# Feed-forward of a hybrid attention block: VectorE makes the inverse of the block scale from the block maximum itself

## The chip, the cores and the metric

One core of a Trainium2 chip runs the whole kernel. The metric is the device time of one execution in microseconds (us). The core has five engines that run their own instruction streams and meet at semaphores: TensorE (PE in the profile; PEld is its weight load), VectorE (DVE), ScalarE (ACT), GpSimd (POOL) and SyncE (SP), which starts the transfers.

## The reference

The input x has 2 x 2048 tokens of 128 channels. Four stages follow, each added to x behind a layer norm: an attention with landmarks, the feed-forward, a linear attention, and the same feed-forward again. The change touches the two feed-forwards alone:

```
def fp4_quant_dequant(x):                       # blocks of 16 along the last dim
    scale = jnp.max(jnp.abs(xb), axis=-1, keepdims=True) / 6.0
    scale = jnp.maximum(scale, jnp.float32(1e-12))
    xn = xb / scale
    idx = jnp.searchsorted(_MID, jnp.abs(xn))   # nearest value of a grid of 8
    q = _GRID[idx] * jnp.sign(xn) * scale

gate = fp4_linear(x, w_gate)                    # both operands quantised
y = fp4_linear(x, w_up)
h = jax.nn.silu(gate) * y                       # 352 wide
return fp4_linear(h, w_down)
```

## The kernel before

The tokens are 32 tiles of 128 tokens (a token on each partition), which stay in SBUF in X. A feed-forward, `ffn(p)` for p = 0 (the first pass) and p = 1 (the second), quantises x by quads of four tiles (8 quads, 512 columns, 32 blocks for a partition) and h by pairs of two tiles (16 pairs, 2 x 352 columns, 44 blocks). All engines walk the same loop over rounds r from -4 to 18; in round r VectorE works on pair r, POOL on the products of pair r - 1, TensorE on the down products of pair r - 2, and in an even round with q = (r + 4) / 2 below 8 the quad q is begun, in the odd round behind it moved on. So x quads are worked on up to r = 11, and in r = 12 to 15 there is h alone.

For one pair the steps are: TensorE's gate and up products (L1234, L1236), ScalarE's silu (L546), VectorE's product (`gated`, L876) into the PSUM bank of up. Then VectorE's block maximum (`absmax_h`, L880) into `hblk[:, 0]`; POOL's scale (`scales`, L254), maximum / 6 but at least 1e-12, into `hblk[:, 2]`; VectorE's reciprocal of it (`inverse`, L841) into `hblk[:, 1]`; VectorE's ratio (`ratio_h`, L886) in PSUM; ScalarE's offset |ratio| x 2^22 in bf16 (`offset_h`, L572); VectorE's clamp of the offset from below (`clamp`, L862, bf16, SBUF to SBUF) and its addition of ratio and offset (`move_h`, L895); in the next round, on POOL, the subtraction of the offset, which leaves the rounded value (`quantise_h`, L271), and the product with the scale (L274). TensorE transposes (L1247), ScalarE copies (L553), TensorE multiplies by w_down (L1255), and the residual is added: in pass 0 by POOL (L279) after a copy by ScalarE (L560), in pass 1 by VectorE straight from PSUM (L899). An x quad goes the same way: `absmax_x` (L849), L254, L841, `ratio_x` (L856), L566, L862, L869, and on POOL `quantise_x` (L261, L264).

The order of each engine is written out in its loop. VectorE in round r: gated twice, absmax_h; absmax_x (even) or clamp and move_x (odd); the residual of pair r - 2 in pass 1; inverse and ratio of h; inverse and ratio of x (even); layernorm statistics of two tiles in pass 0 (L664, L666); clamp and move_h. POOL in round r: the scale of x (even), the scale of h, quantise_h(r - 1), quantise_x (odd), then in pass 0 the residual of pair r - 3 and, in even rounds, four small layernorm steps (L326, among them a power). Semaphore counts order the engines; each step waits for what it reads and for whoever still reads what it overwrites.

Of the kernel before, what the change touches and what calls it, by code (L numbers as in the profile page):

```python
# [16 lines left out]
ALU = mybir.AluOpType  # L17
# [37 lines left out]
TIE = 1.0 - 2.0 ** -23  # L55
# [3 lines left out]
def build(nc, x_d, wqkv_d, wqkvT_d, band_d, wfc_d, bfc_d, wattn_d, battn_d, wproj_d, bproj_d,  # L59
          wg_d, wu_d, wd_d, eye_d, scaled_eye_d, tri_d, blockmask_d, headones_d, rowhead_d, valid_d, centre_d, out_d):  # L60
    with ExitStack() as ctx:
# [9 lines left out]
        s = Signals()  # L71

        def need(eng, name, value):

            if not (isinstance(value, int) and value <= 0):
                eng.wait_ge(s[name], value)
# [111 lines left out]
        def ffn_tiles(p, n):  # L188

            return p * TILES + n  # L190

        def ffn_pairs(p, n):

            return p * PN + n

        def ffn_quads(p, n):

            return p * QN + n
        def up_banks(r):

            return ps[:, 1 + 2 * (r % 2):3 + 2 * (r % 2), 0:F]
# [453 lines left out]
        def _(v):  # L655
            tt, ts, stt = nc.vector.tensor_tensor, nc.vector.tensor_scalar, nc.vector.scalar_tensor_tensor
            reduce, copy, recip = nc.vector.tensor_reduce, nc.vector.tensor_copy, nc.vector.reciprocal
# [24 lines left out]
            def by_block(t):  # L682
# [10 lines left out]
                op0=ALU.mult, op1=ALU.mult).then_inc(s["w_chain"], 1)  # L693
# [10 lines left out]
            for c in range(4):  # L704
                last = copy(out=a2[32 * c:32 * c + 32, :, :],
                            in_=ps[32 * c:32 * c + 32, c % 2, 0:U * M].rearrange("p (u m) -> p u m", m=M))
# [40 lines left out]
            with v.Fori(0, ITERS) as i:  # L747
# [9 lines left out]
                for hf in range(2):  # L757
                    v.wait_ge(s["zT_done"], 2 * i + hf + 1)
                    ts(out=zT[:, 4 * hf:4 * hf + 4, :], in0=banks(6 + hf, 1, P), scalar1=0.25, scalar2=None,
                       op0=ALU.mult).then_inc(s["zT_copied"], 1)  # L760
# [71 lines left out]
            def ffn(p):  # L832
                def pair(t):
                    return t.rearrange("p (k n) -> p k n", k=2)

                def blocks(t):
                    return t.rearrange("p k (b j) -> p k b j", j=BLK)

                def inverse(name, b, n):
                    v.wait_ge(s[name + "_scale"], n + 1)  # L840
                    recip(out=b[:, 1, :], in_=b[:, 2, :]).then_inc(s[name + "_inverse"], 1)  # L841

                def x_blocks():
                    return ps[:, X_BANK:X_BANK + 1, :]

                def absmax_x(q):
                    n = ffn_quads(p, q)
                    v.wait_ge(s["fx_norm"], n + 1)
                    reduce(out=xblk[:, 0, :].unsqueeze(1), in_=blocks(x_blocks()), axis=AX, op=ALU.max,  # L849
                           apply_absolute_value=True).then_inc(s["fx_absmax"], 1)  # L850

                def ratio_x(q):
                    n = ffn_quads(p, q)
                    inverse("fx", xblk, n)
                    v.wait_ge(s["fx_inverse"], n + 1)
                    stt(out=blocks(x_blocks()), in0=blocks(x_blocks()), scalar=TIE,  # L856
                        in1=xblk[:, 1, :].unsqueeze(1).unsqueeze(3).broadcast_to([P, 1, QD * P // BLK, BLK]), op0=ALU.mult,
                        op1=ALU.mult).then_inc(s["fx_ratio"], 1)

# [17 lines left out]

                def absmax_h(r):
                    v.wait_ge(s["f_h"], ffn_tiles(p, 2 * r + 2))
                    reduce(out=pair(hblk[r % 2][:, 0, :]), in_=blocks(up_banks(r)), axis=AX, op=ALU.max,  # L880
                           apply_absolute_value=True).then_inc(s["fh_absmax"], 1)

                def ratio_h(r):
                    n = ffn_pairs(p, r)
                    v.wait_ge(s["fh_inverse"], n + 1)
                    stt(out=blocks(up_banks(r)), in0=blocks(up_banks(r)), scalar=TIE,  # L886
                        in1=pair(hblk[r % 2][:, 1, :]).unsqueeze(3).broadcast_to([P, 2, F // BLK, BLK]), op0=ALU.mult,
                        op1=ALU.mult).then_inc(s["fh_ratio"], 1)

# [12 lines left out]
                for r in range(-FILL, PN + (4 if p == 0 else 3)):  # L902
                    q = (r + FILL) // 2
                    if 0 <= r < PN:
                        gated(2 * r)
                        gated(2 * r + 1)
                        absmax_h(r)
                    if r % 2 == 0 and q < QN:
                        absmax_x(q)
                    if r % 2 and q < QN:  # L910
                        move_x(q)
                    if p == 1 and 0 <= r - 2 < PN:
                        residual(r - 2)
                    if 0 <= r < PN:
                        inverse("fh", hblk[r % 2], ffn_pairs(p, r))
                        ratio_h(r)
                    if r % 2 == 0 and q < QN:
                        ratio_x(q)
                    if p == 0 and 0 <= r - 4 < PN:
                        v.wait_ge(s["f_x_done"], ffn_pairs(p, r - 3))  # L920
                        tile_stats(2, 2 * r - 8)
                        tile_stats(2, 2 * r - 7)
                    if 0 <= r < PN:
                        move_h(r)
# [497 lines left out]
```

## Time and profile before

| what | value |
|---|---|
| median of 3 runs | 854.62 us (854.15 to 855.4) |
| the profiled execution | 855.14 us, of which the span from the first to the last instruction is 853.3 us |
| busy over the span | PE 620.8 us (73%), PEld 445.2 (52%), DVE 543.6 (64%), ACT 296.9 (35%), POOL 317.6 (37%) |
| chain that ended last | PE 46%, DVE 30%, issue 10%, POOL 8%, ACT 5% |
| granted clock of TensorE | 0.873 of full speed |
| feed-forward of pass 0 | from about 384 to 516 us |
| feed-forward of pass 1 | from about 718 us to the end |

How to read it: one execution was recorded, and a busy engine is not yet one that bounds. The two feed-forwards are a third of the time, and which engine is late there has to be read from their own stretches. In a row of the timeline stand the start (us from the span's beginning), the duration, the engine, the source line, the operation, output <- inputs with their shapes, and in brackets how long the engine stood idle before it and for whom. A duration holds whatever an instruction stood still for once it was issued, so a longer one for the same shape tells of something outside of it.

### The profile page before, as it was taken

To read this page: it belongs to the slowest core of one execution; us is meant where nothing else is said; L and a number is where in the kernel's file an instruction comes from. 1 tells how busy PE (TensorE), PEld (TensorE's weight loads), DVE (VectorE), ACT (ScalarE), POOL (GpSimd) and SP (SyncE) were. 2 spreads that over 40 slices of the span, in tenths; PEclk is the share of its full clock that TensorE was granted. 3 is DMA by queue.
4 is the path that set the end of the run, shared out by engine and by line. 5 is a ranking of instruction groups with operands and counts; after the bars stand their busy time and mean duration, and the time that the engine had idled before them with its cause. 6 is when DMAs were issued, how large, how long until landed. Compare 5 with 4: busy or idle time off the path is not lost.

```text
span 853.3 us, 14006 instructions
## 1 busy us (share of the span) xinstructions
PE 620.8 (73%) x5231; PEld 445.2 (52%) x5231; DVE 543.6 (64%) x1078; ACT 296.9 (35%) x523; POOL 317.6 (37%) x408
## 2 busy tenths in 40 slices
PE   2467887888667477694777766698988985777675
PEld 1366784666434344692555544355655653455554
DVE  7624663333198498475889881376667765688874
ACT  2131112333243233204555542233333333545542
POOL 6540000000100000043678876345555534456654
PEclk9567999999988788797899985599999998799997
DMA  8400000000000000000000000000000000000000
GB/s 251 107 1 1 0 1 1 0 1 0 1 2 0 1 1 1 1 1 0 1 1 1 1 1 0 1 1 3 2 1 2 2 2 2 0 13 26 13 25 25
DMA packets 13675, 10.47 MB, mean 12 GB/s; under 512 B 1398, under 2 KB 12598, under 8 KB 13492
## 3 DMA queue, kind: packets, MB, share of 16 engines
q1 hardware_dynamic: 13620, 9.73, 4.1%
q8 instruction: 35, 0.57, 0.3%
q14 instruction: 20, 0.16, 0.1%
HBM read 7.63 MB, written 2.10 MB: 11 GB/s over the span
## 4 chain that ended last, share of the span: by engine, by line
PE 46%; DVE 30%; issue 10%; POOL 8%; ACT 5%; DMA 0%; ACTq 0%; DVEq 0%; POOLq 0%
PE ps L1098 6%; PE ps L1184 4%; PE ps L1318 4%; PE ps L1213 4%; PE ps L1125 3%; DVE ps L876 3%; PE ps L1337 3%; DVE r L786 2%; PE ps L1255 2%; DVE ps L886 2%; DVE hblk L880 2%; DVE hoff L862 2%; PE ps L1134 2%; DVE S L794 2%; PE ps L1142 2%
## 5 line engine op out<-in xcount | busy, mean ns | idle before, releaser
L1247 PE MATMUL ps<-eye,arena 128*128 128x128 f32 (+1 forms) x192 | 32.4, 312 | 56.4 <-POOL arena L274 56.4
L326 POOL TENSOR_TENSOR ln<-mv,lnc 128x4 f32<-128x4 f32 x64 | 13.2, 207 | 155.7 <-DVE mv L666 155.7
L345 POOL MEMSET early<- 128x2560 f32 x2 | 4.5, 2232 | 173.1 <-PE ps L1169 162.0
L1184 PE MATMUL ps<-G,xw 128*126 128x512 f32 x72 | 46.4, 797 | 30.1 <-ACT xw L498 22.4
L374 POOL TENSOR_SCALAR_AFFINE_SELECT arena<-arena 128x1024 f32<-128x1024 f32 x32 | 35.0, 1093 | 78.4 <-ACT arena L623 78.4
L1247 PEld LDWEIGHTS ps<-eye,arena 128*128 128x128 f32 (+1 forms) x192 | 22.9, 150 | 73.4 <-POOL arena L274 72.8
L1255 PEld LDWEIGHTS ps<-wdT,arena 128*128 128x128 f32 (+1 forms) x384 | 53.4, 213 | 14.9 <-ACT arena L553 9.3
L1236 PE MATMUL ps<-wguT,arena 128*128 128x352 f32 x128 | 55.5, 519 | 7.1 <-DVE arena L895 7.1
L1255 PE MATMUL ps<-wdT,arena 128*128 128x128 f32 (+1 forms) x384 | 55.1, 298 | 3.9 <-ACT arena L553 3.7
L1234 PE MATMUL ps<-wguT,arena 128*128 128x352 f32 x128 | 55.3, 517 | 1.8 <-ACT arena L540 1.4
L977 DVE TENSOR_TENSOR arena<-ps,tri 128x1024 f32<-128x1024 f32 x32 | 39.2, 1224 | 25.8 <-PE ps L1318 25.8
L623 ACT ACTIVATE arena<-ps 128x1024 f32<-128x1024 f32 x32 | 32.8, 1024 | 53.3 <-PE ps L1318 53.2
L271 POOL TENSOR_TENSOR arena<-arena,hoff 128x704 f32<-128x704 f32 x32 | 48.6, 1518 | 4.0 <-DVE arena L895 1.6
L274 POOL TENSOR_TENSOR arena<-arena,hblk 128x704 f32<-128x704 f32 x32 | 44.3, 1384 | 2.5
L1194 PEld LDWEIGHTS ps<-band,A 126*32 126x32 f32 x1152 | 32.3, 122 | 24.5 <-DVE A L811 21.0
L1194 PE MATMUL ps<-band,A 126*32 126x114 f32 x1152 | 35.4, 287 | 12.7 <-DVE A L811 12.7
L1098 PE MATMUL ps<-arena 128*128 128x128 f32 x288 | 37.4, 290 | 9.1 <-DVE arena L750 7.4
L503 ACT ACTIVATE S<-S 126x512 f32<-126x512 f32 x36 | 21.9, 630 | 60.9 <-DVE S L794 60.9
L1184 PEld LDWEIGHTS ps<-G,xw 128*126 128x126 f32 x72 | 15.8, 234 | 51.3 <-issue 47.4
L664 DVE BATCH_NORM_STATS2 stats<-X 128x6 f32<-128x128 f32 x128 | 35.3, 276 | 11.1 <-POOL X L279 7.4
L786 DVE TENSOR_REDUCE r<-ps 126x48 f32<-126x1536 f32 x12 | 21.1, 1755 | 33.5 <-PE ps L1184 33.3
L1098 PEld LDWEIGHTS ps<-arena 128*128 128x128 f32 x288 | 35.2, 199 | 11.2 <-DVE arena L750 8.5
(194 smaller groups left out, 1543.1 us busy)
## 6 DMA issues: line engine op xcount, KB each, us to landing
X<-in_x SPq DMA_DIRECT2D x8, 256.0 KB, 4.8
out<-X SPq DMA_DIRECT2D x8, 256.0 KB, 2.3
wqkv<-in_wqkv SPq DMA_DIRECT2D x1, 1024.0 KB
band<-in_band SPq DMA_DIRECT2D x1, 897.8 KB
early<-in_wfc SPq DMA_DIRECT2D x1, 512.0 KB
kI<-in_scaled_eye SPq DMA_DIRECT2D x1, 192.0 KB
wattn<-in_wattn SPq DMA_DIRECT2D x1, 192.0 KB, 7.5
S<-in_wd SPq DMA_DIRECT2D x1, 176.0 KB, 3.2
```

The lines of the kernel that those rows point to most:

```text
L271: tt(out=hgrid, in0=hmoved[k], in1=hoff[k][:, :], op=ALU.subtract).then_inc(s["fh_grid"], 1)
L274: tt(out=blocks(hquant[k].rearrange("p k n -> p (k n)")), in0=blocks(hgrid), in1=hblk[k][:, 2, :].unsqueeze(2).broadcast_to([P, 2 * F // B ...
L664: nc.vector.bn_stats(out=stats[:, t, :], in_=X[:, t, :]).then_inc(s["stats_raw"], 1)
L786: reduce(out=r1[:, 0, :], in_=psf[0:WI, 0:NW * HM].rearrange("p (k m) -> p k m", m=M), axis=AX, op=ALU.max).then_inc(s["s1_max"], 1)
L977: tt(out=masked[n % 2][:, 0:8, :], in0=psf[:, 0:2 * QW].rearrange("p (h t) -> p h t", t=P), in1=tri[:, :].unsqueeze(1).broadcast_to([P, 8, ...
L1098: last = mm(banks(bank + hf, 1, P)[:, u, :], lhsT[:, 4 * hf + u, :], rhs[:, 4 * hf + u, :], start=True, stop=True)
L1184: last = mm(ps[0:WI, w, :], xw[:, w * WO:w * WO + WI], G1[:, b, :], start=True, stop=True)
L1194: last = mm(ps[32 * c:32 * c + 32, 4 + g, w * WO:(w + 1) * WO], A1v[:, w, h * M:(h + 1) * M], band[:, h, :], start=True, stop=True)
L1234: mm(ps[:, GATE_BANK, 0:F], x, wguT[:, 0:F], start=True, stop=True).then_inc(s["f_gate"], 1)
L1236: mm(up_banks(r)[:, t % 2, :], x, wguT[:, F:2 * F], start=True, stop=True).then_inc(s["f_up"], 1)
L1247: last = tp(ps[0:FK[c], T_BANK + k, c * P:(c + 1) * P], hquant[r % 2][:, k, c * P:c * P + FK[c]], eye[:, :])
L1255: last = mm(ps[:, T_BANK + 1, k * P:(k + 1) * P], hT[r % 2][0:FK[c], k, c, :], wdT[0:FK[c], c, :], start=(c == 0), stop=(c == 2))
```

## The change

VectorE's `inverse` no longer waits for POOL's scale. It waits for its own block maximum, takes the larger of it and 6e-12 with a tensor_scalar into `b[:, 1]`, waits for that, and takes the reciprocal of `b[:, 1]` in place. The inverse is then 1 / maximum, not 6 / maximum, and the factor 6 goes into the constant of the ratio. The semaphore of the inverse counts two for each use. POOL's scale stays as it is and is read only by POOL's own product. Since VectorE no longer waits for the scale before it goes on, each block maximum now waits until the previous scale from the same buffer has been made.

```diff
                 def inverse(name, b, n):
-                    v.wait_ge(s[name + "_scale"], n + 1)
-                    recip(out=b[:, 1, :], in_=b[:, 2, :]).then_inc(s[name + "_inverse"], 1)
+                    v.wait_ge(s[name + "_absmax"], n + 1)
+                    ts(out=b[:, 1, :], in0=b[:, 0, :], scalar1=6e-12, scalar2=None, op0=ALU.max).then_inc(s[name + "_inverse"], 1)
+                    v.wait_ge(s[name + "_inverse"], 2 * n + 1)
+                    recip(out=b[:, 1, :], in_=b[:, 1, :]).then_inc(s[name + "_inverse"], 1)
...
                 def absmax_x(q):
                     n = ffn_quads(p, q)
                     v.wait_ge(s["fx_norm"], n + 1)
+                    need(v, "fx_scale", n)
...
                     inverse("fx", xblk, n)
-                    v.wait_ge(s["fx_inverse"], n + 1)
-                    stt(out=blocks(x_blocks()), in0=blocks(x_blocks()), scalar=TIE,
+                    v.wait_ge(s["fx_inverse"], 2 * n + 2)
+                    stt(out=blocks(x_blocks()), in0=blocks(x_blocks()), scalar=6.0 * TIE,
...
                 def absmax_h(r):
                     v.wait_ge(s["f_h"], ffn_tiles(p, 2 * r + 2))
+                    need(v, "fh_scale", ffn_pairs(p, r - 1))
...
                 def ratio_h(r):
                     n = ffn_pairs(p, r)
-                    v.wait_ge(s["fh_inverse"], n + 1)
-                    stt(out=blocks(up_banks(r)), in0=blocks(up_banks(r)), scalar=TIE,
+                    v.wait_ge(s["fh_inverse"], 2 * n + 2)
+                    stt(out=blocks(up_banks(r)), in0=blocks(up_banks(r)), scalar=6.0 * TIE,
```

## Rows read from the trace of the kernel before

**Rows 1.** Stages: stretch, length, busy us of each engine, clock, DMA share, GB/s

```profile
412.00:484.00 72.00, 54.86 (x281) 39.43 (x280) 63.20 (x126) 39.81 (x86) 55.40 (x65) 0.91 0.00 1
...
746.00:812.00 66.00, 47.52 (x266) 34.49 (x266) 57.47 (x98) 34.36 (x72) 40.59 (x42) 0.97 0.06 17
```

**Rows 2.** Timeline, all engines, second pass, r = 7: start, us, engine, line

```profile
784.41 1.52 POOL L271 TENSOR_TENSOR arena<-arena,hoff 128x704 f32<-128x704 f32 x1
...
784.99 0.42 DVE L841 RECIPROCAL hblk<-hblk 128x44 f32<-128x44 f32 x1
...
786.01 1.38 POOL L274 TENSOR_TENSOR arena<-arena,hblk 128x704 f32<-128x704 f32 x1
...
787.16 0.43 DVE L862 TENSOR_SCALAR hoff<-hoff 128x704 bf16<-128x704 bf16 x1 [0.82 <-ACT hoff L572]
...
787.35 1.26 POOL L261 TENSOR_TENSOR arena<-arena,xoff 128x512 f32<-128x512 f32 x1
```

**Rows 3.** Timeline, all engines, second pass, r = 6

```profile
777.87 0.43 DVE L841 RECIPROCAL hblk<-hblk 128x44 f32<-128x44 f32 x1 [0.33 <-POOL hblk L254]
...
777.91 1.52 POOL L271 TENSOR_TENSOR arena<-arena,hoff 128x704 f32<-128x704 f32 x1
...
779.13 0.34 DVE L841 RECIPROCAL xblk<-xblk 128x32 f32<-128x32 f32 x1
...
779.51 1.38 POOL L274 TENSOR_TENSOR arena<-arena,hblk 128x704 f32<-128x704 f32 x1
...
780.12 0.97 DVE L862 TENSOR_SCALAR hoff<-hoff 128x704 bf16<-128x704 bf16 x1
```

**Rows 4.** Timelines of DVE and of POOL, first pass, even and odd round

```profile
446.64 0.85 DVE L862 TENSOR_SCALAR hoff<-hoff 128x704 bf16<-128x704 bf16 x1
...
451.05 0.42 DVE L841 RECIPROCAL hblk<-hblk 128x44 f32<-128x44 f32 x1
...
453.22 0.77 DVE L862 TENSOR_SCALAR hoff<-hoff 128x704 bf16<-128x704 bf16 x1
...
446.56 0.73 POOL L279 TENSOR_TENSOR X<-X,arena 128x256 f32<-128x256 f32 x1
...
450.81 1.52 POOL L271 TENSOR_TENSOR arena<-arena,hoff 128x704 f32<-128x704 f32 x1
...
452.41 1.38 POOL L274 TENSOR_TENSOR arena<-arena,hblk 128x704 f32<-128x704 f32 x1
```

**Rows 5.** Groups of DVE by shape: busy us, mean ns, idle before

```profile
L959 DVE TENSOR_SCALAR arena<-ps 128x64 f32<-128x64 f32 x8 | 1.8, 224 | 16.7 <-PE ps L1301 16.7
...
L687 DVE TENSOR_SCALAR blk<-blk 128x70 f32<-128x70 f32 x1 | 0.2, 199 | 0.0
...
L996 DVE TENSOR_SCALAR bias_qk<-bias_qk 128x2 f32<-128x2 f32 x1 | 0.2, 151 | 0.0
```

**Rows 6.** One line, the clamp of h: duration ns min/median/max, first and last start

```profile
L862 DVE TENSOR_SCALAR hoff<-hoff x32: 332/762/1045, 403.9 to 840.7; 128x704 bf16<-128x704 bf16 x32
```

**Rows 7.** One line, L671, and the timeline of 14 to 26 us

```profile
L671 DVE TENSOR_SCALAR arena<-X,ln x32: 314/340/346, 7.3 to 25.6; 128x128 f32<-128x128 f32 x32
...
15.56 1.01 POOL L326 TENSOR_TENSOR ln<-ln,lnc 128x4 f32<-128x4 f32 x1
```

**Rows 8.** Groups of DVE by shape: the two reciprocals

```profile
L841 DVE RECIPROCAL hblk<-hblk 128x44 f32<-128x44 f32 x32 | 13.5, 423 | 10.7 <-POOL hblk L254 10.7
...
L841 DVE RECIPROCAL xblk<-xblk 128x32 f32<-128x32 f32 x16 | 5.5, 345 | 3.2 <-POOL xblk L254 3.2
```

**Rows 9.** Timeline of DVE, the first pass's first quad

```profile
387.26 0.35 DVE L841 RECIPROCAL xblk<-xblk 128x32 f32<-128x32 f32 x1 [1.68 <-POOL xblk L254]
```

**Rows 10.** Timelines of DVE and of POOL, second pass, r = 12

```profile
819.22 0.42 DVE L841 RECIPROCAL hblk<-hblk 128x44 f32<-128x44 f32 x1
...
821.39 0.70 DVE L862 TENSOR_SCALAR hoff<-hoff 128x704 bf16<-128x704 bf16 x1 [0.82 <-ACT hoff L572]
...
818.90 1.52 POOL L271 TENSOR_TENSOR arena<-arena,hoff 128x704 f32<-128x704 f32 x1
```

## The prediction

> **What bounds the kernel now.** I read the busy time of each engine by stage first, since the change touches only the two feed-forward passes (384 to 516 us and 718 to 853 us). In their steady parts VectorE is busy for 63.2 of 72 us and 57.5 of 66 us, more than any other engine, and POOL (the GpSimd engine) comes second in the first [rows 1]. The chain of waits runs there along VectorE's own order, round after round, and changes over to POOL in places. So the next view is the timeline of one round of each kind, VectorE beside POOL.
>
> An odd round of the second pass, r = 7, lasts from 781.93 to 788.44 us. What the reader is to see in it [rows 2]: POOL's subtraction at L271 starts at 784.41 and holds POOL to 785.93. VectorE's reciprocal (L841) starts inside it, at 784.99, for the scale was ready long before (it was made while VectorE did the x quad's clamp and addition). The clamp of the h offsets (L862) starts at 787.16, waited for ScalarE, and takes 0.43; it ends at 787.59, 0.20 us after POOL's product L274 (786.01 + 1.38 = 787.39). POOL's next instruction, L261, ends at 788.61.
>
> The even round before it [rows 3]: the reciprocal starts at 777.87, after VectorE has stood idle for 0.33 us for POOL's scale (L254), and the clamp, begun at 780.12, takes 0.97: it ends at 781.09, again 0.20 us behind L274 (779.51 + 1.38 = 780.89). That round's end is POOL's: scale, L271, L274, then the clamp. In the first pass it is alike, but one product later: the clamp of 446.64 ends at 447.49, 0.20 us behind POOL's residual addition L279 (446.56 + 0.73 = 447.29), which got in ahead of it [rows 4].
>
> **The clamp tells of a lock.** Over its 32 executions the clamp takes 332 to 1045 ns for the same shape [rows 6]. Where POOL streams through a 704-column or 256-column operation it never ends earlier than 0.20 us after that operation, and where POOL is free it takes 0.33. So a VectorE tensor_scalar from SBUF to SBUF in its fast form stands still while POOL works on such tensors. It goes first, though, ahead of a POOL instruction that is queued behind the running one: L261 is recorded from 787.35, before the clamp's end, and takes 1.26 [rows 2]. The reciprocal has no such spread: it takes 0.42 or 0.43 in each row shown, inside L271 or not [rows 2 to 4], with a mean of 423 ns [rows 8]. It doesn't take part.
>
> **What the change does, part by part.** It adds 48 instructions to VectorE, a maximum with a constant over 44 columns (32 of them) or 32 columns (16), ahead of each reciprocal. Is that one of the fast form, and so of those that stand still? The trace has three short tensor_scalars: 2 columns 151 ns, 70 columns from SBUF 199 ns, 64 columns from PSUM 224 ns [rows 5]. From PSUM that is 1.1 ns for a column more, from SBUF 0.7, below the one cycle that a column costs in the slow form. I therefore take the new instruction as a fast one: 0.18 us of its own (151 + 42 x 0.7 ns), 0.21 with the 0.03 us gap behind it, and liable to be held by POOL. Bounds from the nearest rows: as cheap as 0.18 if nothing holds it, as dear as 1.05 us, the longest clamp. That POOL doesn't hold everything is seen early on: L671, a tensor_scalar over 128 columns, takes 314 to 346 ns in all 32 cases, though many run inside POOL's power step of 1.01 us, which touches 4 columns [rows 7]. I take the long products to hold the port and the 4-column steps not to.
>
> The Trainium skill ("SBUF — State Buffer", Who interferes with whom) says that a VectorE tensor_scalar which qualifies for a two-port mode and a GpSimd instruction exclude each other for the whole instruction, whichever starts first; the clamp's rows agree, and L671's inside the power step don't. By the page to the letter the gain at the first start below would be some 0.6 us smaller, and the sum larger by as much.
>
> It removes VectorE's waits for POOL's scale, 10.7 us before the h reciprocals and 3.2 us before those of x [rows 8]. It adds a wait for the previous scale ahead of each absmax: POOL made that scale a quad or two pairs earlier, before products which have since been waited for, so it costs nothing. The scale, no longer VectorE's, is still the first thing in POOL's order. The constants (6 x TIE, 6e-12) cost nothing.
>
> *Odd rounds with an x quad (r = 1 to 11, 6 in each pass).* Nothing was waited for here, so nothing is gained. The new instruction reaches VectorE where the reciprocal stood, 784.99, inside L271, and is held to 785.93. With 0.04 for itself (held, it needs less behind the release than alone, as the clamp needs 0.20 for 0.33) and the gap the reciprocal starts at 786.00, 1.01 later; ratio, ScalarE's offset and so the clamp follow, 787.16 + 1.01 = 788.17. By then L274 has ended (787.39) and L261 is under way, which the clamp used to get ahead of. It now waits for its end: 788.61 + 0.20 = 788.81 in place of 787.59, 1.22 us more [rows 2]. In the first pass the reciprocal of 451.05 moves to 452.40 (L271 ends at 452.33), which brings the clamp of 453.22 to 454.57, again past L274 and into L261 [rows 4]. So 12 x 1.22 = 14.6 us. All POOL's work stays on its old times in such a round; its idleness grows.
>
> *Even rounds with an x quad (r = 2 to 10, 5 in each pass).* The h reciprocal comes up to 0.7 us earlier, but the x one is now preceded by an instruction that falls into L271 (777.91 to 779.43), and starts at 779.50, not 779.13 [rows 3]. The clamp is reached at 780.49, still before L274 ends, and ends where it did. In the first pass it is still reached before L279 ends [rows 4]. Zero, with up to 0.1 each if the new instruction gets ahead of POOL's scale and delays it.
>
> *The last four rounds of the second pass (r = 12 to 15).* No x quad. L271 runs from 818.90 to 820.42, and the reciprocal moves from 819.22 to 820.49, 1.27 later. The clamp moves from 821.39 to 822.66; POOL has nothing behind L274 now, so it takes 0.33 and ends at 822.99 in place of 822.09 [rows 10]. 4 x 0.90 = 3.6 us. In the first pass there is no residual on VectorE between absmax and reciprocal, the new instruction comes before L271, and the clamp is bound by L274 as before: zero.
>
> *Starts.* At the first quad of the first pass the reciprocal waited 1.68 us, for POOL was at the layernorm steps [rows 9]. That wait goes, less 0.24 for the instruction and its gaps: -1.4. The second pass's start gives back 0.3 of the waits in rows 8. At r = 0 of each pass POOL has no products yet; the idle 0.95 goes, two new instructions come: -0.5 each. Together -2.7.
>
> Sum: 14.6 + 3.6 - 2.7 = +15.5 us. The profiled execution took 855.14 us (span 853.3), which would give 870.6; that is 0.5 above the median of 854.62, from which I forecast **870.1**.
>
> **Rivals.** *One: POOL doesn't hold so short an instruction.* For it: L671 passes the power step unharmed, and 199 ns is one sample between 187 (half a cycle a column) and 222. Then odd rounds lose nothing, because the clamp waits for L274's end anyhow (0.2 later of 0.23 to be had, rows 2), the tail hides it too, and in four even rounds of the first pass the clamp gets in ahead of L279, which it missed by 0.08 us: 447.29 - 446.56 = 0.7 each. -2.7 - 2.8 = -5.5: **849.1**, faster. *Two: the new instruction is held for part of the time only,* 0.5 us, say. In the second pass the clamp still slips past L274 (from 0.23 us on), in the first, where it began 0.57 us before L274's end, it doesn't: 6 x 1.22 + 4 x 0.2 - 2.7 = +5.4, **860**. *Three: lock and slip as forecast, and TensorE cools.* Its granted clock is 0.91 and 0.97 of full in the steady parts [rows 1], and rounds longer by 1.2 us leave it idle for longer; the second pass's residual waits for it. Each such dip would add about a microsecond, three to six of them: **874**. *Four: nothing measurable,* rival one with its gains lost again in ScalarE's and TensorE's waits: **853.5**.
>
> **Chances.** Forecast 0.66, rival three 0.12, two 0.06, one 0.12, four 0.04. The range goes from 860 to 876, which holds the first three. 0.2% of the time (1.7 us) is about what a measurement of this kernel can tell from no change: faster 0.13, same 0.03, slower 0.84.
>
> **What the profile will show.** If right: a new group of 32 on hblk whose mean is far over 0.18 us, near 1 us in odd rounds, each ending some 0.04 us after L271; the clamp of odd rounds ending 0.20 us after L261, no longer after L274; odd rounds of 7.7 us and even ones of the second pass of 7.5 as now; the reciprocal without idleness before it; the first x ratio 1.4 us earlier. Wrong if the new group's longest is under 0.3 us: then it is rival one. If it is held but the clamp still starts before L274's end, the slip is the wrong step.

## The result, and the profile after

| | before | after |
|---|---|---|
| median, runs side by side | 855.01 us (854.15 to 855.99, 4 runs) | 872.73 us (871.72 to 873.24, 4 runs) |
| the profiled execution | 855.14 us, span 853.3 | 873.16 us, span 871.4 |
| busy VectorE, POOL | 543.6, 317.6 us | 570.0, 316.2 us |
| granted clock of TensorE | 0.873 | 0.864 |

The change costs 2%: the ratio is 1.0202 (95% interval 1.0189 to 1.0214). The forecast was 870.1 us in a range of 860 to 876. The profiled execution became 18.0 us longer; the sum had said 15.5.

The page of after, its line of the span and those of busy time, and the shares of the chain that ended last:

```profile
span 871.4 us, 14099 instructions
...
PE 633.7 (73%) x5231; PEld 450.6 (52%) x5231; DVE 570.0 (65%) x1126; ACT 295.4 (34%) x523; POOL 316.2 (36%) x408
...
PE 46%; DVE 34%; issue 10%; POOL 5%; ACT 5%; DMA 0%; ACTq 0%; DVEq 0%; POOLq 0%
```

VectorE is busy for 26.4 us more, with 48 instructions more, and its share of the chain rose from 30 to 34%. The new instruction alone accounts for 31.2 us. Durations of one line (ns, min/median/max; first and last start), and the same groups of VectorE by shape (busy us, mean ns, idle before):

```profile
L841 DVE TENSOR_SCALAR hblk<-hblk x32: 175/772/1416, 399.8 to 856.2; 128x44 f32<-128x44 f32 x32
L841 DVE TENSOR_SCALAR xblk<-xblk x16: 170/181/1153, 385.4 to 819.0; 128x32 f32<-128x32 f32 x16
...
L841 DVE TENSOR_SCALAR hblk<-hblk 128x44 f32<-128x44 f32 x32 | 23.1, 723 | 0.1
...
L841 DVE TENSOR_SCALAR xblk<-xblk 128x32 f32<-128x32 f32 x16 | 8.1, 507 | 0.1
```

The same 44 columns take 0.175 us at best and 1.416 at worst. What holds them is seen best in an odd round. This is r = 3 of the second pass, all engines; rows 2 are its like of before:

```profile
758.45 1.52 POOL L271 TENSOR_TENSOR arena<-arena,hoff 128x704 f32<-128x704 f32 x1
...
759.03 0.99 DVE L841 TENSOR_SCALAR hblk<-hblk 128x44 f32<-128x44 f32 x1
...
760.05 0.43 DVE L843 RECIPROCAL hblk<-hblk 128x44 f32<-128x44 f32 x1
...
760.05 1.38 POOL L274 TENSOR_TENSOR arena<-arena,hblk 128x704 f32<-128x704 f32 x1
...
761.39 1.16 POOL L261 TENSOR_TENSOR arena<-arena,xoff 128x512 f32<-128x512 f32 x1
...
762.24 0.51 DVE L865 TENSOR_SCALAR hoff<-hoff 128x704 bf16<-128x704 bf16 x1 [0.82 <-ACT hoff L572]
```

The maximum starts inside POOL's L271 and ends at 760.02, 0.05 us behind it. Everything behind it is late, and the clamp (now L865) ends at 762.75, 0.20 us behind L261 (761.39 + 1.16 = 762.55), no longer behind L274. In words: the held maximum makes the clamp late, the late clamp finds the next POOL product under way and is held a second time. The round lasts 7.61 us where the undisturbed one of before lasted 6.50.

The round lengths, each from one round's first product on VectorE (L876, now L879) to that of the next:

| stretch | before | after | difference |
|---|---|---|---|
| up to round 1 of the first pass | | | -1.4 |
| odd rounds r = 1 to 11, first pass | 6.42 to 6.56 | 7.54 to 7.62 | +6.6 in all |
| even rounds r = 2 to 10, first pass | 7.50, four of 8.18 | 7.50, three of 8.18, one 8.64 | +0.5 |
| r = 12 to 14, first pass | | | -0.7 |
| between the passes (r = 15 of the first to r = 0 of the second) | 225.4 | 222.8 | -2.5 |
| r = 0, second pass | 8.78 | 7.35 | -1.4 |
| odd rounds r = 1 to 11, second pass | five of 6.5, one 7.81 | four of 7.6, two 8.90 | +7.9 |
| even rounds r = 2 to 10, second pass | 7.49 to 7.50 | 7.50, four of 8.72 | +4.9 |
| r = 12 to 14, second pass | 6.50 | 7.45, 7.45, 8.91 | +4.3 |

The sum is 18.2 us, the difference of the spans 18.1. Two of the rows are not as forecast: the even rounds of the second pass, which were to cost nothing, and the stretch between the passes, nearly all of which is code that the change leaves alone. The first has a cause in TensorE's clock. Stretches of the two kernels' second passes (stretch, length, busy us of PE, PEld, DVE, ACT, POOL, clock, DMA share, GB/s), before and after:

```profile
746.00:816.00 70.00, 49.60 (x276) 35.80 (x276) 60.54 (x104) 35.58 (x74) 44.43 (x45) 0.98 0.07 20
```
```profile
746.00:830.00 84.00, 62.22 (x283) 43.49 (x281) 69.83 (x122) 38.13 (x82) 46.33 (x47) 0.86 0.06 16
```

The granted clock is 0.98 before and 0.86 after. It isn't evenly lower: from the end of r = 1 to r = 14 after has eight short stretches, 30.7 us together, at the lower of the clock's two levels (1.2 GHz, half of 2.4), where before has a single one between 742 and 841 us, in its 7.81 round. Each of the seven rounds of 8.7 and 8.9 us of after has one (the eighth, in r = 12, did no harm), and the even round without one, r = 6, lasts 7.50. This is r = 4 with its stretch (763.5 to 766.9), all engines:

```profile
765.06 2.37 PE L1259 MATMUL ps<-wdT,arena 128*128 128x128 f32 x12
...
767.06 1.52 POOL L271 TENSOR_TENSOR arena<-arena,hoff 128x704 f32<-128x704 f32 x1
...
767.47 0.43 DVE L903 TENSOR_TENSOR X<-ps,X 128x256 f32<-128x256 f32 x1 [1.41 <-PE ps L1259]
...
767.81 0.81 DVE L841 TENSOR_SCALAR hblk<-hblk 128x44 f32<-128x44 f32 x1
...
768.66 1.39 POOL L274 TENSOR_TENSOR arena<-arena,hblk 128x704 f32<-128x704 f32 x1
...
769.93 0.17 DVE L841 TENSOR_SCALAR xblk<-xblk 128x32 f32<-128x32 f32 x1
...
771.13 0.33 DVE L865 TENSOR_SCALAR hoff<-hoff 128x704 bf16<-128x704 bf16 x1
```

The twelve down products take 2.37 us; in r = 6 of the same trace, at full clock, they take 1.60, as in r = 4 of before. The residual (L903) waits for them for 1.41 us, so the h maximum behind it starts at 767.81, which is no longer ahead of L271 but inside it. It is held until 768.62, and the clamp comes at 771.13, after L274 is done, with 0.33 us. In r = 6 the maximum came at 782.85, 0.54 us before L271 (783.39), and took 0.18:

```profile
782.51 0.42 DVE L903 TENSOR_TENSOR X<-ps,X 128x256 f32<-128x256 f32 x1
...
782.85 0.18 DVE L841 TENSOR_SCALAR hblk<-hblk 128x44 f32<-128x44 f32 x1
...
784.34 0.61 DVE L841 TENSOR_SCALAR xblk<-xblk 128x32 f32<-128x32 f32 x1
...
785.98 0.59 DVE L865 TENSOR_SCALAR hoff<-hoff 128x704 bf16<-128x704 bf16 x1
```

The four even rounds of 8.72 were not equally late. The h maximum starts 4.62, 4.22, 4.31 and 3.62 us into r = 2, 4, 8 and 10, where 2.93 was in time in r = 6; but in all four it ends 5.04 us into the round (5.03 in r = 2), 0.04 us behind L271. The one that was least late was held longest. These are r = 2 and r = 10 (rounds that start at 747.26 and 812.65):

```profile
750.73 1.52 POOL L271 TENSOR_TENSOR arena<-arena,hoff 128x704 f32<-128x704 f32 x1
...
751.88 0.41 DVE L841 TENSOR_SCALAR hblk<-hblk 128x44 f32<-128x44 f32 x1
```
```profile
816.13 1.52 POOL L271 TENSOR_TENSOR arena<-arena,hoff 128x704 f32<-128x704 f32 x1
...
816.27 1.42 DVE L841 TENSOR_SCALAR hblk<-hblk 128x44 f32<-128x44 f32 x1
```

In the two rounds of 8.90, and in r = 14, the late maximum missed even the gap between L271 and L274. Here L274 had been under way since 791.49, and holds the maximum to 792.91 (r = 7):

```profile
791.49 1.39 POOL L274 TENSOR_TENSOR arena<-arena,hblk 128x704 f32<-128x704 f32 x1
...
791.53 0.42 DVE L903 TENSOR_TENSOR X<-ps,X 128x256 f32<-128x256 f32 x1 [1.31 <-PE ps L1259]
...
791.87 1.04 DVE L841 TENSOR_SCALAR hblk<-hblk 128x44 f32<-128x44 f32 x1
```

### The profile page after: what moved, and what is told of

It is laid out like the page before. It is cut to its first block, busy times and chain, and to the rows that moved or that the text cites. A ratio compares the mean times of both kernels' runs of the same rounds, so it can differ in the third digit from the quotient of the medians.

```text
span 871.4 us, 14099 instructions
## 1 busy us (share of the span) xinstructions
PE 633.7 (73%) x5231; PEld 450.6 (52%) x5231; DVE 570.0 (65%) x1126; ACT 295.4 (34%) x523; POOL 316.2 (36%) x408
## 3 DMA queue, kind: packets, MB, share of 16 engines
HBM read 7.63 MB, written 2.10 MB: 11 GB/s over the span
## 4 chain that ended last, share of the span: by engine, by line
PE 46%; DVE 34%; issue 10%; POOL 5%; ACT 5%; DMA 0%; ACTq 0%; DVEq 0%; POOLq 0%
PE ps L1102 6%; PE ps L1188 5%; PE ps L1322 4%; PE ps L1259 4%; PE ps L1217 3%; PE ps L1129 3%; DVE ps L890 3%; PE ps L1341 3%; DVE r L786 2%; DVE hblk L841 2%; DVE ps L879 2%; PE ps L1240 2%; PE ps L1138 2%; DVE S L794 2%; DVE hoff L865 2%
## 5 line engine op out<-in xcount | busy, mean ns | idle before, releaser
L1240 PE MATMUL ps<-wguT,arena 128*128 128x352 f32 x128 | 59.5, 551 | 20.1 <-DVE arena L899 20.1
L1259 PEld LDWEIGHTS ps<-wdT,arena 128*128 128x128 f32 (+1 forms) x384 | 60.3, 237 | 17.2 <-ACT arena L553 11.4
L1259 PE MATMUL ps<-wdT,arena 128*128 128x128 f32 (+1 forms) x384 | 62.1, 324 | 5.3 <-ACT arena L553 5.1
L1238 PE MATMUL ps<-wguT,arena 128*128 128x352 f32 x128 | 56.8, 530 | 2.0 <-ACT arena L540 1.4
L271 POOL TENSOR_TENSOR arena<-arena,hoff 128x704 f32<-128x704 f32 x32 | 48.6, 1518 | 4.0 <-DVE arena L899 1.6
L1240 PEld LDWEIGHTS ps<-wguT,arena 128*128 128x128 f32 x128 | 26.4, 223 | 45.7 <-DVE arena L899 35.3
L274 POOL TENSOR_TENSOR arena<-arena,hblk 128x704 f32<-128x704 f32 x32 | 44.3, 1384 | 2.5
L546 ACT ACTIVATE arena<-ps 128x352 f32<-128x352 f32 x64 | 29.6, 463 | 39.0 <-PE ps L1238 27.8
```

The lines of the kernel that those rows point to most:

```text
L271: tt(out=hgrid, in0=hmoved[k], in1=hoff[k][:, :], op=ALU.subtract).then_inc(s["fh_grid"], 1)
L274: tt(out=blocks(hquant[k].rearrange("p k n -> p (k n)")), in0=blocks(hgrid), in1=hblk[k][:, 2, :].unsqueeze(2).broadcast_to([P, 2 * F // B ...
L1238: mm(ps[:, GATE_BANK, 0:F], x, wguT[:, 0:F], start=True, stop=True).then_inc(s["f_gate"], 1)
L1240: mm(up_banks(r)[:, t % 2, :], x, wguT[:, F:2 * F], start=True, stop=True).then_inc(s["f_up"], 1)
L1259: last = mm(ps[:, T_BANK + 1, k * P:(k + 1) * P], hT[r % 2][0:FK[c], k, c, :], wdT[0:FK[c], c, :], start=(c == 0), stop=(c == 2))
```

## The experiments

The theory: the maximum is a VectorE instruction that stands still while POOL's long products run, and that alone makes the odd rounds and the tail longer. Its rivals: the new order (VectorE no longer waits for POOL's scale) does it, or the instruction's own time, or TensorE's clock. Ratios are to the kernel before on the same chip, with 95% intervals.

**The maximum left out.** Same order, the same wait for the block maximum, no new instruction. (`.then_inc(...)` stands for the count that the full line gives; the two ratios then wait for one count, not two.)

```diff
-                    ts(out=b[:, 1, :], in0=b[:, 0, :], scalar1=6e-12, scalar2=None, op0=ALU.max).then_inc(...)
-                    v.wait_ge(s[name + "_inverse"], 2 * n + 1)
-                    recip(out=b[:, 1, :], in_=b[:, 1, :]).then_inc(s[name + "_inverse"], 1)
+                    recip(out=b[:, 1, :], in_=b[:, 0, :]).then_inc(s[name + "_inverse"], 1)
...
```

> The changed kernel without the maximum with 6e-12: the reciprocal reads the block maximum directly (left out: the lower bound for blocks of all zeros on VectorE's side). VectorE has as many instructions as before the change and no wait for POOL's scale. Theory: what the change saves without what it adds: -1.7 and -0.5 at the starts, -0.7 each at r = 0, four times -0.7 in the first pass, 847 to 850 us. Rival (the removed waits were worth nothing, for POOL's chain ends later anyhow): 853 to 855 us.

Measured: 848.27 us, ratio 0.9910 (0.9893 to 0.9926). So the new order is worth 0.9%, and the 48 maxima cost 24.5 us, of which their own 0.18 us each would be 9; the rest is holding, and what follows from it. Odd rounds are back at 6.50, but for r = 3 of the second pass: it has a stretch at the lower clock from 745.4 us on, and with r = 2 it takes 6.21 + 9.25 us in place of 14.0. Four even rounds of the first pass went from 8.18 to 7.50, for the clamp is now ahead of the residual addition of POOL that it missed by 0.08 us before [rows 4]. Timelines of POOL and VectorE of this kernel, r = 6 of the first pass:

```profile
441.35 1.38 POOL L274 TENSOR_TENSOR arena<-arena,hblk 128x704 f32<-128x704 f32 x1
...
441.73 1.20 DVE L863 TENSOR_SCALAR hoff<-hoff 128x704 bf16<-128x704 bf16 x1
...
442.69 0.83 POOL L279 TENSOR_TENSOR X<-X,arena 128x256 f32<-128x256 f32 x1
```

**The maximum alone, added to before.** It writes a tile that nobody reads; the wait for the scale and everything else stay.

```diff
...
                     v.wait_ge(s[name + "_scale"], n + 1)
+                    v.wait_ge(s[name + "_spare"], n)
+                    ts(out=spare[:, 0:44 if name == "fh" else 32], in0=b[:, 0, :], scalar1=6e-12, scalar2=None, op0=ALU.max).then_inc(s[name + "_spare"], 1)
                     recip(out=b[:, 1, :], in_=b[:, 2, :]).then_inc(s[name + "_inverse"], 1)
```

> The kernel before with the 48 maxima added to it and their result unused: they stand behind the wait for POOL's scale, ahead of the reciprocal, which reads POOL's scale as before. Theory: the added instruction alone makes the whole loss, in odd rounds 1.1 us each by the slip of the clamp, in the second pass's last four 0.9 each, more where TensorE's clock falls, and none of the gains at the starts: 871 to 880 us. Rival (the loss comes from leaving out the wait for the scale, by another order of POOL and VectorE): 855 to 862 us, 48 times 0.2 us at most.

Measured: 874.07 us, 1.0235 (1.0204 to 1.0266). The unused instruction does all the damage by itself, with before's order and waits kept. Durations of its line:

```profile
L843 DVE TENSOR_SCALAR spare<-hblk x32: 185/714/1323, 400.9 to 856.5; 128x44 f32<-128x44 f32 x32
```

**Only h, only x.** The change is made for one of the two tensors; the other keeps its wait for the scale.

```diff
                 def inverse(name, b, n):
+                    if name == "fx":
+                        v.wait_ge(s[name + "_scale"], n + 1)
+                        recip(out=b[:, 1, :], in_=b[:, 2, :]).then_inc(s[name + "_inverse"], 1)
+                        return
...
```

(These are the lines of h alone; x alone has "fh" in the first added line.)

> The change for h alone; the x quads keep POOL's scale. Theory (the loss is the 32 maxima of h, held inside L271, and the clamp that slips behind L261): the loss stays whole, and only the gain at the starts (1.7 and 0.5 us) is missing, 870 to 877 us. Rival (the x maxima of the even rounds, which fall into L271 or L274, carry a good part of it): 862 to 868 us.

> The change for the x quads alone; h keeps POOL's scale. Theory: x's maximum is held to the end of L271 in even rounds, which costs nothing while POOL's chain ends the round, and the starts give 2 us: 851 to 855 us. Rival (as with the h maxima in PSUM, where x's arrived 0.03 us too late and were held through L274 as well, 1.2 us in each such round): 858 to 866 us.

Measured: h alone 871.23 us, 1.0195 (1.0167 to 1.0223); x alone 857.01, 1.0016 (0.9987 to 1.0044). Nearly all of the loss is h's, as its place inside L271 in every odd round says. x alone missed its forecast of 851 to 855 by 2 us. In its profiled execution, with 861.93 us 4.9 above the median, the odd rounds stay at 6.5 but for two (7.63 and 7.81), and two even rounds of the second pass grew to 9.25 and 8.71; each of the four has a stretch at the lower clock in it or just ahead of it. So what the start gives is lost again in single rounds. The 7.63 has this slip of the clamp behind L261 (which starts at 481.85 and ends at 483.01), in VectorE's timeline:

```profile
481.93 1.28 DVE L869 TENSOR_SCALAR hoff<-hoff 128x704 bf16<-128x704 bf16 x1 [0.63 <-ACT hoff L572]
```

**The maximum somewhere else.** Each one right behind its block maximum, which comes before POOL begins L271. The work is that of after; `floor` is the part of `inverse` with the wait for the block maximum and the maximum with 6e-12.

```diff
-                def inverse(name, b, n):
+                def floor(name, b, n):
...
+
+                def inverse(name, b, n):
...
                         absmax_h(r)
+                        floor("fh", hblk[r % 2], ffn_pairs(p, r))
                     if r % 2 == 0 and q < QN:
                         absmax_x(q)
+                        floor("fx", xblk, ffn_quads(p, q))
```

> The changed kernel with one thing moved: each maximum with 6e-12 stands right behind its block maximum, where POOL is idle, not ahead of the reciprocal, where POOL is in L271. Theory (the new instruction is held by POOL's long products, and the clamp then slips behind L261): all 48 of them take under 0.25 us, odd rounds return to 6.5 us, four even rounds of the first pass get the clamp in ahead of the residual (-0.7 us each), the second pass's even rounds lose 0.2 us each, and the time is 849 to 853 us. Rival (the loss is what the 48 instructions and their semaphores cost VectorE by themselves, and TensorE's clock): the place doesn't matter, 868 us or more.

Measured: 857.77 us, 1.0025 (1.0003 to 1.0047). The lock's part of the theory held, the total didn't. Not one of the 48 is held:

```profile
L841 DVE TENSOR_SCALAR hblk<-hblk x32: 185/186/189, 397.9 to 839.8; 128x44 f32<-128x44 f32 x32
L841 DVE TENSOR_SCALAR xblk<-xblk x16: 180/181/182, 384.0 to 806.8; 128x32 f32<-128x32 f32 x16
```

Against after this is 15 us, for moving an instruction by a few places. But it came out above my 849 to 853. Even rounds of the second pass lasted 7.71 and most odd ones 6.62, where before has 7.50 and 6.50: an instruction on VectorE's own path costs its 0.1 to 0.2 us even when nothing holds it, and I had booked that for the even rounds alone. The larger part is another: three odd rounds lasted 7.74 to 7.82 and r = 2 of the first pass 8.68, 4.7 us together over 6.62 and 7.50, each with a stretch at the lower clock in it or just ahead of it. And the stretch between the passes was 1.9 us longer than before's.

**Another destination.** The h maxima write into free columns of the pair's PSUM bank (the new last argument of `inverse`), and the reciprocal reads there; their place is that of the change.

```diff
-                        inverse("fh", hblk[r % 2], ffn_pairs(p, r))
+                        inverse("fh", hblk[r % 2], ffn_pairs(p, r), ps[:, 1 + 2 * (r % 2), 400:444])
...
```

> The changed kernel with the 32 maxima of h written to PSUM (unused columns of the pair's own bank) and read from there by the reciprocal; place, count and order of the instructions are the same. An instruction that writes PSUM takes no fast form. Theory (lock on the SBUF to SBUF fast form): each of the 32 takes 0.2 us though it stands inside L271, odd rounds return to 6.5 to 6.6 us, the x ones in even rounds are still held, 851 to 855 us. Rival (any VectorE instruction of that kind there is slowed while POOL runs, or the added instruction itself is the cost): 868 us or more.

Measured: 864.62 us, 1.0097 (1.0063 to 1.0132), a miss for the total. Durations of the two groups:

```profile
L842 DVE TENSOR_SCALAR ps<-hblk x32: 195/197/207, 399.7 to 849.4; 128x44 f32<-128x44 f32 x32
L842 DVE TENSOR_SCALAR xblk<-xblk x16: 170/613/1389, 385.3 to 816.9; 128x32 f32<-128x32 f32 x16
```

With the result in PSUM none of the 32 is held, in the place where 44 columns from SBUF to SBUF took up to 1416 ns in after; 19 of them start inside L271 or L274. So the destination decides here whether the instruction is held. But x's maxima are still held (the one at 767.22 for 1.39 us, by the L274 of 767.19), and five of the six odd rounds of the second pass stayed long all the same, three at 7.61 or 7.62 and two, with a stretch at the lower clock, at 8.75. This is why, for the three:

```profile
774.90 1.38 POOL L274 TENSOR_TENSOR arena<-arena,hblk 128x704 f32<-128x704 f32 x1
...
776.24 1.16 POOL L261 TENSOR_TENSOR arena<-arena,xoff 128x512 f32<-128x512 f32 x1
...
776.29 1.30 DVE L866 TENSOR_SCALAR hoff<-hoff 128x704 bf16<-128x704 bf16 x1 [0.82 <-ACT hoff L572]
```

L274 ended at 776.28, the clamp was there at 776.29, and L261 had gone first. 0.23 us of slack [rows 2] are used up by a maximum of 0.20 us and its gap of 0.03. Missed by 10 ns, the clamp pays 1.1 us.

**TensorE's clock.** Eight products of the identity (their result is overwritten) keep TensorE at work while it would wait for POOL's product of h. Added to after and to before.

```diff
-                    pe.wait_ge(s["fh_quant"], n + 1)
                     need(pe, "fx_T_copied", ffn_quads(p, min((r + 5) // 2, QN)))
                     need(pe, "fh_T_copied", 2 * n)
+                    for k in range(8):
+                        mm(ps[:, T_BANK, 384:512], eye[:, :], eye[:, :], start=True, stop=True)
+                    pe.wait_ge(s["fh_quant"], n + 1)
```

> The changed kernel, with eight products of the identity added on TensorE ahead of its wait for POOL's product in every round of h, where it stands idle (their result is overwritten). Theory (four even rounds and two odd ones of the second pass lost 1.2 and 2.4 us since TensorE's clock was at half in them and the residual on VectorE came late): the granted clock stays at full through both passes, those rounds return to 7.5 and 7.6 us, 862 to 867 us. Rival (the residual is late for the order of TensorE's work, whatever its clock): 871 us or more.

> The kernel before with the same eight products. It had few rounds at half clock in the feed-forwards, one of 7.8 us in the second pass in place of 6.5: 851 to 855 us by the theory. If the added products themselves delay the transposes behind them, 857 us or more, and the run on the changed kernel has to be read against this one.

Measured: 862.34 us, 1.0100 (1.0058 to 1.0143), and 850.42 us, 0.9950 (0.9932 to 0.9968), the second just below its forecast. The products give 10.4 us to after and 4.6 to before. Stretches of their second passes, after with them and before with them:

```profile
735.00:833.00 98.00, 88.60 (x558) 70.34 (x558) 87.56 (x149) 46.06 (x96) 57.07 (x56) 0.98 0.06 17
```
```profile
735.00:825.00 90.00, 85.96 (x557) 70.83 (x558) 77.84 (x132) 45.82 (x96) 57.68 (x56) 0.98 0.06 19
```

The clock is 0.98 in both. Inside the passes the change now does what the sum said and nothing else: the 12 odd rounds go from 6.51 to 7.62, all even rounds of the second pass are 7.50 in both, r = 12 to 14 of it go from 6.51 to 7.45. Without the stretch between the passes and the end (from r = 15 of the second pass on) that is +13.9 us, and it is the lock's part without the clock's. The whole pair differs by less, 10.9 us in the profiled executions and 11.9 by the medians (17.7 without the products), since with the change the stretch between the passes is 4.6 us shorter and the end 1.6 longer, neither of which the sum had.

**Both remedies.** One kernel without the maxima and with the products; and one with the whole computation, where the maxima stand behind the last block maximum of the round (x's first, then h's) and TensorE has the products.

```diff
...
                         absmax_x(q)
+                        floor("fx", xblk, ffn_quads(p, q))
+                    if 0 <= r < PN:
+                        floor("fh", hblk[r % 2], ffn_pairs(p, r))
```

> The kernel without the maximum with 6e-12 (left out: the lower bound for blocks of all zeros on VectorE's side), and the eight products of the identity on TensorE. Theory: the two gains are of different places and add up, 0.9% from the one and 0.5% from the other: 842 to 846 us. Rival (in the kernel without the maximum TensorE's clock was at full in all but one round of the passes already, so nothing is left to gain and the eight products are in the way): 847 to 850 us.

> The changed kernel complete, with each maximum behind the last block maximum of its round, that of x ahead of that of h, so that POOL's scale of x isn't made to wait, and with the eight products on TensorE. Theory: no maximum is held by POOL's products (the h one in even rounds by POOL's short scales at most, 0.6 us), odd rounds 6.6 us, even ones 7.5 us in both passes, starts 1.6 us earlier: 845 to 850 us, below the kernel before with the same eight products. Rival (0.2 us of each maximum stays on VectorE's path in 32 rounds): 852 us or more.

Measured: 843.68 us, 0.9861 (0.9831 to 0.9892), and 847.15 us, 0.9907 (0.9877 to 0.9937). The second computes all that the reference wants and is faster than both kernels, 8.3 us below the before measured beside it (855.49) and 25.6 below after. None of its 48 maxima is held:

```profile
L841 DVE TENSOR_SCALAR hblk<-hblk x32: 177/186/190, 400.1 to 830.7; 128x44 f32<-128x44 f32 x32
L841 DVE TENSOR_SCALAR xblk<-xblk x16: 181/181/183, 385.5 to 797.6; 128x32 f32<-128x32 f32 x16
```

Its even rounds are 7.50 and its odd ones 6.63, but for three early ones of the first pass. About half of the gain over before is the products', though: before with them is at 850.42, 3.3 us above it, and the intervals of the two ratios overlap by a little (0.9932 to 0.9937). That this kernel beats before with the same products is likely, not shown.

## Why the prediction was right, and where it was not

**The lock: right.** In every held case the maximum ends 0.04 or 0.05 us behind the POOL product (760.02 against 759.97), as the working had it. In r = 3 it puts the reciprocal off by 1.02 us (0.99 and the gap of 0.03), where 1.01 was worked out. It was argued from the clamp's rows [rows 2 to 4, 6]. Two runs now show it without the rest of the change: the unused maximum alone costs 2.35%, and without the maxima the change gains 0.9%. The Trainium skill ("SBUF — State Buffer", Who interferes with whom) has the same rule, that a tensor_scalar in a two-port mode and a GpSimd instruction exclude each other for the whole instruction. Its long products agree. The 4-column power step doesn't: the first quad's maximum runs inside it at 385.39 and takes 0.18 us. Taken to the letter the page would have cost 0.6 us there, which the trace of after doesn't show; that 4-column steps hold nothing was the working's choice, and it held. Its reason was weak, though: L671 takes 340 ns for 128 columns [rows 7], by the working's own 151 ns for 2 columns 1.5 ns for each further one, twice the 0.7 of its fast form, so L671 passing the power step says little of that form. (The slope from PSUM is 1.2 ns a column, 73 over 62, not 1.1; nothing hangs on it.) These rows do:

```profile
385.14 1.01 POOL L326 TENSOR_TENSOR ln<-ln,lnc 128x4 f32<-128x4 f32 x1
...
385.39 0.18 DVE L841 TENSOR_SCALAR xblk<-xblk 128x32 f32<-128x32 f32 x1
...
385.61 0.35 DVE L843 RECIPROCAL xblk<-xblk 128x32 f32<-128x32 f32 x1
```

POOL's scale holds nothing either, with 44 columns in 0.36 us. The maximum of r = 15 runs inside it in 0.17 us:

```profile
856.12 0.36 POOL L254 TENSOR_SCALAR hblk<-hblk 128x44 f32<-128x44 f32 x1 [5.49 <-DVE hblk L884]
...
856.21 0.17 DVE L841 TENSOR_SCALAR hblk<-hblk 128x44 f32<-128x44 f32 x1
```

L279 with 256 columns holds the clamp [rows 4]. Where between 44 and 256 columns the hold begins, and whether it goes by length or by kind of instruction, no run tells.

**The slip of the clamp behind L261: right, its size was 1.11 us, not 1.22.** The clamp ends 0.20 us behind L261 in the 12 odd rounds but for the two where the maximum itself was held through L274. The 1.22 took L261's end from rows 2 (788.61), where its 1.26 us hold 0.1 us of waiting for the clamp, which had got in ahead. Unhindered it takes 1.16. Twelve times 1.11 is 13.3 in place of 14.6.

**The tail: right in kind, wrong in number.** r = 12 and 13 grew by 0.95 and 0.96 (forecast 0.90), and in the warm pair all of r = 12 to 14 did. r = 15 did not: it takes 5.65 in both, since its maximum comes before L271 is under way, and its clamp ends behind L274 in both. The term was 2.8, not 3.6. That r = 14 grew by 2.4 is again the clock.

**Starts: right in sum** (-3.1 for -2.7), not in each part. At the first quad the time from block maximum to ratio fell from 2.72 to 1.30 us, the 1.4 booked; another 0.2 came from ahead of it. But r = 0 of the first pass went from 7.91 to 8.19, a loss of 0.3 where 0.5 was to be gained. The second pass's start gave 0.3, as booked (from 5.73 to 5.45 us between its first two block maxima of x), and its r = 0 went from 8.78 to 7.35, 1.4 where 0.5 was booked; in the warm pair it went from 8.31 to 7.49, 0.8.

**Even rounds of the first pass: right.** Zero, but for r = 10, where the clamp came behind L279 (+0.5) after a stretch at half clock.

**Even rounds of the second pass: the step that failed.** The prediction booked them at zero because the h maximum came before L271 and the x one's delay was hidden by L274. That was true at full clock alone: in r = 6 of after and in every one of the warm pair. It left out that the h maximum is only 0.54 us ahead of L271, and that the residual in front of it waits for TensorE. Rival three had this (TensorE cools, "about a microsecond, three to six of them"), with a chance of 0.12; its 874 us is as a mechanism what happened, and nearer to the measured 872.7 than the forecast is. It happened seven times in the second pass: +1.22 for four even rounds, +1.29 for two odd ones beyond their 1.11, +1.46 for r = 14 beyond 0.95, together 8.9 us, from which goes the 1.3 of before's own such round. The mechanism has a second half that the rival lacked: the lock turns different latenesses into one fixed price. The h maximum was 0.7 to 1.7 us late in the four even rounds, and each round costs 1.22, since the maximum ends behind L271 whichever of them it was. An estimate from r = 4: were no maximum held, x's would start 1.31 us after h's end, at 769.30, and the clamp 1.20 after that, at 770.50, and end with its 0.33 at 770.83, not at 771.46. That is 0.6 later into the round than in r = 6, for 0.7 of the 1.3 us of lateness is to spare behind L274. By the same working r = 10, 0.7 us late, would have cost nothing and r = 2, 1.7 us late, 1.0. So TensorE's share of such a round's price runs from none of it to 1.0 us, and the lock has the rest.

**Why the total was only 2.6 us off.** The odd rounds and the tail were booked 2.1 us too dear, 2.2 of the 2.5 us that came back between the passes were forecast by nothing, the starts gave 0.4 more than booked, and 1.3 came with before's own slow round; against them stand 8.9 us of the clock (the table's +0.5 and -0.7 of the first pass nearly cancel). So the closeness of 870.1 to 872.7 is in part luck: errors of both signs cancel. The working proper is borne out by the rounds of the warm pair alone, with +13.9 us where the corrected terms give 13.3 + 2.8 - 2.7 = 13.4.

**What stays open: the 2.5 us between the passes.** Of these 0.3 are the gain at the second pass's start; for the rest the code is the same in all kernels but for TensorE's added products and r = 15, whose clamp ends after 5.66 us in each. Its length ranges from 219.4 (after with the products) over 221.6, 222.8, 224.0, 225.4 (before) to 227.9 (x alone). Part of what a kernel gains or loses against another by the median lies there, and none of the runs was made for it. TensorE's clock goes with it: the granted clock of 500 to 720 us is 0.91 in the shortest, 0.89, 0.88, 0.89, 0.85 in the next four, and 0.82 in the longest. That it is the cause is not shown, nor what sets the clock there. The stretch blurs each of the comparisons above by a few us, the 3.3 us between the last kernel and the warm before among them.

**The other rivals.** Rival one (no hold, 849.1) is out; its price is near that of the kernel that has nothing to hold, 848.3, which hasn't the 48 instructions either. But its sentence that odd rounds lose nothing, "0.2 later of 0.23 to be had", was too thin, as the PSUM kernel showed by 10 ns. Rival two (held for a part) is out: each held case goes to the end of POOL's product. Rival four is out by the result.

## What to carry to other kernels

Taking away a wait for another engine at the price of one small instruction is a good trade only where that instruction can't be locked out: look what POOL does at the very time it is issued, and count it at the length of POOL's longest product, not at its own (here up to 1.42 us for 0.18). Before that, look for a place on the same engine where POOL is idle; here some places earlier in VectorE's order turned +2.0% into +0.25%, and feeding TensorE on top made it -0.9%, of which before too gets 0.5% by the feeding. And a small slack ahead of a lock isn't one: 0.23 us went by 10 ns, and 0.54 us didn't outlast TensorE at half clock. A step whose lateness is priced by a lock costs nothing or a microsecond, so ask of each engine ahead of it how late it can be.

## What the runs showed of the hardware that was not expected

- A VectorE tensor_scalar on f32 is held however short it is: 32 columns took 0.17 us free and 1.39 held. Written to PSUM instead of SBUF, 44 columns took 195 to 207 ns in 32 cases, held in none. The reciprocal isn't held: h's took 427 to 430 ns in all 32 cases of after, that of 760.05 with L274 beside it all the time. Beside POOL's steps of 4 columns (1.01 us) and of 44 columns (0.36 us) the maximum took its free 0.17 to 0.18 us.
- A held VectorE instruction goes ahead of the POOL instruction queued behind the one that holds it, and a short one is over 0.04 us after the release, against 0.20 for the clamp's 704 columns. In the PSUM kernel's three cases where POOL was first by 0.05 or 0.06 us (776.24 against 776.29, for one) POOL had it for the whole 1.16 us.
- Ahead of each of its eight half-clock stretches in after TensorE had stood idle for 1.65 to 2.85 us, six times for L274 and twice for VectorE's L899 (1.99 us before 761.49, for instance). But so it had in r = 5, for 2.00 us, with no stretch behind it, and before stands idle for 2.25 us in three rounds at full clock. What selects the rounds stays open. Eight small products put into that idleness brought the granted clock of the second pass from 0.86 to 0.98 in after, and gave 10.4 us to after and 4.6 to before.
